# Two graph attention layers: another order of a step's parts in the first layer, and the node update's sum and copies moved

## The chip, the cores and the metric

The kernel runs on one core of a Trainium2 chip. The metric is the device time of one execution in microseconds. The median of three runs of the kernel before is 4821.75 us (4820.29 to 4824.06).

A core has five engines with an instruction queue each: TensorE (PE, matrix products and transposes), VectorE (DVE), ScalarE (ACT), GpSimd (POOL; here it issues the gathers) and SyncE (SP; here it issues all other transfers). In each queue the instructions stand in the order in which the program wrote them, and an instruction that waits for a semaphore holds back all that stand behind it in its queue. The transfers themselves are done by 16 DMA engines.

## The reference, cut to what matters

12500 nodes with 256 features, 200000 edges sorted by their destination, an edge type out of 64.

```python
# layer 0: attention over the incoming edges, 4 heads of 64
enh = x + 0.1 * query_emb
Q, K, V = enh @ Wq + bq, enh @ Wk + bk, enh @ Wv + bv
mod_k = K[src] + 0.2 * rel_w[edge_type]
scores = sum(Q[dst] * mod_k) / 8                 # per edge and head
w = softmax of scores over the edges of one dst
msgs = sum over edges of w * V[src]              # V itself for a node without edges
x1 = layernorm(msgs @ Wo + bo + x) * gamma + beta
x = layernorm(x + x1)
# layer 1: graph attention with a self loop, again 4 heads of 64
xp = x @ W;  a_src, a_dst = per head xp . att_src, xp . att_dst
w = softmax of leaky_relu(a_src[src] + a_dst[dst]) over the edges and the loop of one dst
x = layernorm(x + elu(sum of w * xp[src] + bias))
```

## The kernel before, in words

The kernel has four stages: tables made from the edge list, projection of the nodes to queries, keys and values, `attend_typed` (layer 0) and `attend_plain` (layer 1). The change touches `attend_typed` only.

The edges are cut into 521 tiles of 384 (three chunks of 128; a tile's scores also take the first 32 edges of the next one, the "spill"). A tile has up to 32 destination nodes. Every engine has a loop over steps, and in step t it handles a different part of several tiles. A `TilePart(lag, fn)` in a list calls fn for tile t - lag. The order in which the parts of a step stand in an engine's queue is the order of that list. TensorE's parts are:

- `relate` (lag 0): a one-hot of the edge types times the relation table, into `p_r`.
- `arrive` (lag 1): waits for the three gathers of the tile, then six transposes of key rows into `p_kt` (line 851).
- `turn_weights` (lag 5): transposes the softmax weights (lines 859, 860).
- `score` (lag 3): keys times queries (line 874). It needs the keys of the next tile too, because of the spill.
- `aggregate` (lag 6): weights times value rows (line 889). It frees the tile's row buffer.

GpSimd's `gather` (line 765) issues three indirect transfers per tile into one of eight row buffers. It first waits until `aggregate` of the tile eight places back is done. VectorE's parts are `add_keys` (lines 963, 964: relations added to the turned keys; the keys go to a ring of four tiles), `copy_weights` (line 972, for odd tiles; ScalarE does the even ones), `prepare` (line 980, the one-hot) and `lower_bound` (lines 991, 993: scores less a far mask, and their maximum). ScalarE's are `copy_relations` (1147), `copy_weights` (1155), `set_apart` (1140, the far mask), `weigh` (1160, the exponential) and `put` (1167, the sums to their store). `p_kt`, `p_r`, `p_s`, `p_w` and `p_o` hold one tile each. VectorE's numbers run two steps ahead of TensorE's, ScalarE's one: with TensorE's step s goes VectorE's s + 2.

Beside the tiles, 98 blocks of 128 nodes get their node update. `BlockPart(shift, lag, fn)` calls fn in the step that lies `shift` behind a block's place; the places are 4, 4 and 8 steps apart, three in 16 steps. Block parts stand behind the tile parts of their step. TensorE's part is `update(v)`, which stands ahead of a step's tile parts, one step behind each place. It handles three blocks at once: the output projection of one (lines 902, 904, into `p_out`), the second layer's projection of another (905, 907, into `p_1`), and the transposes of a third's message and a fourth's finished row (915, 917, into `p_message` and `p_x1`). `p_out` and `p_x1` share a bank. VectorE's block parts are `join` (999 to 1005, the message), `sum_up` (1017 to 1024, residual sum and its statistics), `normalize` (1052, 1054), `vary` (1060 to 1065, second statistics), `end_norm` (1073), and the inverse root of three blocks' variances (341 to 348). ScalarE's are `copy_message` (1172), `copy_x1` (1179), `copy_row` (1189 to 1191) and `keep_x1` (1183). After the last tile the block parts run on alone until the last blocks are through.

Of the kernel before, what the change touches and what calls it, by code (L numbers as in the profile page):

```python
# [290 lines left out]
def interleave(eng, first, *parts):  # L291


    assert (TILES - first) % PERIOD == 0

    def step(t):
        for part in parts:
            part.at(t)

    for n in range(first):  # L300
        step(Step(0, n, PERIOD))
    with eng.Fori(0, (TILES - first) // PERIOD) as q:
        for c in range(first, first + PERIOD):
            step(Step(q, c, PERIOD))
    for n in range(TILES, max(part.end() for part in parts)):
        step(Step(0, n, PERIOD))
# [371 lines left out]
def attend_typed(k):  # L678
# [3 lines left out]
    R, M, KEY, SCORE, TURN_LAG, LAG = 8, 4, 1, 3, 5, 6  # L682
    WEIGHTS = 12
    W1 = D + 2 * HEADS
    FIRST = 89
    HALF = PERIOD // 2
    PE_FIRST = 9
    with Stage(nc, "typed") as z:
# [62 lines left out]
        TURN, OUT, TURN1, PROJECT = 2, 3, 10, 11  # L751
# [85 lines left out]
        def _(pe):  # L837
# [55 lines left out]
            def update(v, n, static=False):  # L893


                within = lambda lag: not static or v - lag < ROWS
                pe.wait_ge(row1_ready, v + 1)
                pe.wait_ge(x1_t_ready, v + 1)
                if within(OUT):
                    pe.wait_ge(message_t_ready, v + 1)  # L900
                    pe.wait_ge(summed, v + 1)
                    pe.matmul(p_out, ones[:], bias_o[:], start=True, stop=False)
                    for a in range(2):
                        pe.matmul(p_out, message_t[:, a * P:a * P + P], wo[:, a], start=False, stop=a == 1)
                pe.matmul(p_1, ones[:], bias_1[:], start=True, stop=False)
                for a in range(2):
                    last = pe.matmul(p_1, x1_t[:, a * P:a * P + P], w1[:, a], start=False, stop=a == 1)
                last.then_inc(moved, 1)
                if within(TURN1):
                    pe.wait_ge(x1_ready, v + 1)  # L910
                    if within(TURN):
                        pe.wait_ge(message_ready, v + 1)
                        pe.wait_ge(result_ready, TILES if static else n - LAG)
                        for a in range(2):
                            pe.transpose(p_message[:, a * P:a * P + P], message[:, a * P:a * P + P], ident)
                    for a in range(2):
                        last = pe.transpose(p_x1[:, a * P:a * P + P], x1[:, a * P:a * P + P], ident)
                    last.then_inc(turned_both, 1)

            parts = (TilePart(0, relate), TilePart(KEY, arrive), TilePart(TURN_LAG, turn_weights), TilePart(SCORE, score))  # L920

            def step(t, copied=None):
                for part in parts:
                    part.at(t)
                TilePart(LAG, lambda b: aggregate(b, copied)).at(t)

            pe.wait_ge(setup, 1)
            for n in range(PE_FIRST):
# [25 lines left out]
        def _(v):  # L954
# [52 lines left out]

            def sum_up(b):
                o = b.slot(GROUP)
                v.wait_ge(moved, b.n + OUT + 1)  # L1010
                if not b.known_below(1):
                    back = b.back(-2)
                    if not back.known_below(GROUP):
                        v.wait_ge(inverse, back.use(GROUP))
                if not b.known_below(GROUP):
                    v.wait_ge(normed, b.n - 2)
                v.tensor_tensor(y[:, o], p_out, k.node_rows(b.n), ALU.add).then_inc(summed, 1)
                v.wait_ge(summed, b.n + OUT + 2)
                v.bn_stats(stats[:, 0], y[:, o]).then_inc(stats1, 1)
                v.wait_ge(stats1, b.n + 1)  # L1020
                v.sem_inc(settled3, 1)
                v.bn_aggr(moments[:, 0, o], stats[:, 0]).then_inc(moments1, 1)
                v.wait_ge(moments1, b.n + 1)
                v.tensor_scalar(var[:, 0, o:o + 1], moments[:, 0, o, 1:2], 1e-5, 0.5, ALU.add, ALU.mult).then_inc(var1, 1)
# [95 lines left out]
            for side in range(2):  # L1120
# [4 lines left out]
            v.sem_inc(summed, OUT + 1)  # L1125
            v.sem_inc(x1_ready, TURN1)
            v.sem_inc(setup, 1)
            interleave(v, FIRST, TilePart(KEY + 2, add_keys), TilePart(TURN_LAG + 2, copy_weights), TilePart(0, prepare), TilePart(SCORE + 2, lower_bound),
                       BlockPart(3, 8, end_norm), BlockPart(3, 5, normalize), BlockPart(6, 5, vary), BlockPart(4, 2, sum_up), BlockPart(5, 0, join),
                       BlockPart(7, 0, guess_root, ROWS + 8), BlockPart(8, 0, refine_root, ROWS + 8))  # L1130

        @block.scalar
        def _(act):
# [67 lines left out]
            for lo in range(0, P, REL):  # L1201
                for half in range(2):
# [2 lines left out]
            act.sem_inc(x1_t_ready, PROJECT)  # L1205
            act.sem_inc(row1_ready, PROJECT + 1)
            act.wait_ge(setup, 1)
            interleave(act, FIRST, BlockPart(2, 1, copy_message), TilePart(1, copy_relations), TilePart(TURN_LAG + 1, copy_weights), TilePart(SCORE, set_apart), TilePart(SCORE + 1, weigh), TilePart(LAG + 1, put),
                       BlockPart(4, 10, copy_row), BlockPart(4, 9, copy_x1), BlockPart(5, 8, keep_x1))


def attend_plain(k):
# [1720 lines left out]
```

## Time and profile before

| | us |
|---|---|
| median of 3 runs | 4821.75 |
| the profiled execution's own time | 4847.24 |
| its span | 4845.9 |
| TensorE busy, mean granted clock | 4004.0 (83%), 0.868 |
| VectorE busy | 3436.6 (71%) |
| ScalarE busy | 2781.9 (57%) |
| GpSimd busy | 3127.0 (65%) |
| first and last gather of the first layer | 351.1, 2666.0 |
| first gather of the second layer | 2747.3 |

The shares are means over stages that differ, so a change to one layer is read from that layer's stretch. Busy time of TensorE includes time at half clock, when the same matmul takes longer.

### The profile page before, as it was taken

The page shows a single profiled execution, that of the slowest core. Times are in us where ns is not written, and L with a number is a line of the kernel's source. Part 1 is how long each engine was busy: PE and PEld are TensorE (multiplying, and loading weights), DVE is VectorE, ACT ScalarE, POOL GpSimd, SP SyncE. Part 2 cuts the span into 40 slices and gives each one's busy share as a digit, 9 for nine tenths or more (in the row PEclk, how much of TensorE's full clock was granted, in tenths as well). Part 3 has the DMA queues.
Part 4 walks back from the last instruction along what each step waited for, and adds up shares of the span by engine and source line. Part 5 has one row for each costly group of instructions (what it writes and reads, how often), then busy time and mean ns, then how long its engine had stood idle before and what let it go on. Part 6 is the DMA issues. An engine that isn't in the chain of part 4 may idle for free. (4 is left out here: it accounts for less than half of the span.)

```text
span 4845.9 us, 149801 instructions
## 1 busy us (share of the span) xinstructions
PE 4004.0 (83%) x42462; PEld 2592.5 (53%) x42462; DVE 3436.6 (71%) x11602; ACT 2781.9 (57%) x7985; POOL 3127.0 (65%) x3229
## 2 busy tenths in 40 slices
PE   6978889889998888988889688777788777777785
PEld 4645545555555555555555456555565555555553
DVE  3235667677777777777777568888887787777887
ACT  2324444445454455445545367777777777777775
POOL 1226666666666666666666277777777777777773
PEclk9989999999999999999999677877767887888776
DMA  6878888888888888888888377777777777777774
GB/s 207 282 225 232 236 224 226 231 236 234 235 243 231 234 240 241 231 240 239 232 237 237 101 193 208 206 207 206 208 208 205 207 207 204 204 203 206 205 205 131
DMA packets 820558, 1052.06 MB, mean 217 GB/s; under 512 B 458633, under 2 KB 632338, under 8 KB 820464
## 3 DMA queue, kind: packets, MB, share of 16 engines
q0 software_dynamic: 225072, 726.83, 51.5%
q1 hardware_dynamic: 594078, 323.35, 26.7%
q10 hardware_dynamic: 1314, 0.99, 0.1%
q14 instruction: 80, 0.66, 0.0%
q8 instruction: 14, 0.23, 0.0%
HBM read 915.79 MB, written 133.39 MB: 217 GB/s over the span
## 5 line engine op out<-in xcount | busy, mean ns | idle before, releaser
L765 POOL DMA_INDIRECT typed_rows<-kv,typed_index x1563 | 1491.3, 954 | 857.4 <-PE typed_p_o L889 420.3
L1288 POOL DMA_INDIRECT plain_rows<-xp,plain_index x1563 | 1563.2, 1000 | 556.3 <-issue 437.2
L1140 ACT ACTIVATE typed_far<-typed_match,all_cst 128x416 bf16<-128x416 uint8 x521 | 334.2, 642 | 1002.2 <-DVE typed_col L991 983.8
L1393 PE MATMUL plain_p_o<-plain_rows,plain_weight_t 128*64 128x130 f32 (+1 forms) x8336 | 864.3, 350 | 49.5 <-DVE plain_weight_t L1419 48.8
L1380 PE MATMUL plain_p_s<-all_cst,plain_rows 128*128 128x128 f32 (+1 forms) x2084 | 453.9, 317 | 362.0 <-DMA plain_rows<-xp,plain_index 360.2
L1393 PEld LDWEIGHTS plain_p_o<-plain_rows,plain_weight_t 128*64 128x64 f32 (+1 forms) x8336 | 574.2, 170 | 212.0 <-issue 131.7
L851 PE MATMUL typed_p_kt<-all_cst,typed_rows 128*128 128x128 f32 x3126 | 473.8, 290 | 255.8 <-DMA typed_rows<-kv,typed_index 254.9
L964 DVE TENSOR_TENSOR typed_kt<-typed_p_kt,typed_rel 128x768 f32<-128x768 f32 x521 | 497.0, 954 | 230.7 <-PE typed_p_kt L851 202.2
L1380 PEld LDWEIGHTS plain_p_s<-all_cst,plain_rows 128*128 128x128 f32 (+1 forms) x2084 | 334.9, 173 | 515.1 <-issue 497.4
L851 PEld LDWEIGHTS typed_p_kt<-all_cst,typed_rows 128*128 128x128 f32 x3126 | 345.1, 145 | 359.1 <-DMA typed_rows<-kv,typed_index 299.0
L1426 DVE CUSTOM_DVE_ANT_0 plain_alpha<-plain_alpha,plain_far 128x416 f32<-128x416 f32 x521 | 310.6, 596 | 313.1 <-ACT plain_alpha L1542 299.9
L889 PEld LDWEIGHTS typed_p_o<-typed_rows,typed_weight_t 128*32 128x32 f32 (+1 forms) x16672 | 289.7, 111 | 435.7 <-issue 302.2
L874 PE MATMUL typed_p_s<-typed_kt,typed_q 64*32 64x416 f32 x4168 | 505.5, 558 | 0.0
L1550 ACT ACTIVATE plain_weight<-plain_alpha,plain_col 128x416 f32<-128x416 f32 x521 | 331.6, 636 | 249.5 <-DVE plain_col L1435 242.2
L1561 ACT COPY plain_result<-plain_p_o 32x65 f32<-32x65 f32 x2084 | 423.4, 203 | 18.4
L889 PE MATMUL typed_p_o<-typed_rows,typed_weight_t 128*32 128x65 f32 (+1 forms) x16672 | 427.3, 230 | 1.6 <-ACT typed_result L1167 1.5
L1365 PE MATMUL plain_p_w<-all_cst,plain_weight 128*128 128x128 f32 x1563 | 361.6, 352 | 48.1 <-ACT plain_weight L1550 47.4
L1542 ACT ACTIVATE plain_alpha<-plain_p_s,plain_a_dst 128x416 f32<-128x416 f32 x521 | 316.3, 607 | 124.9 <-PE plain_p_s L1380 102.7
L1419 DVE COPY plain_weight_t<-plain_p_w 128x512 f32<-128x512 f32 x521 | 355.5, 682 | 34.8 <-PE plain_p_w L1366 25.2
L1533 ACT ACTIVATE plain_far<-plain_match,all_cst 128x416 bf16<-128x416 uint8 x521 | 328.6, 631 | 9.1 <-DMA plain_match<-match 9.1
L991 DVE CUSTOM_DVE_ANT_0 typed_weight<-typed_p_s,typed_far 128x416 f32<-128x416 f32 x521 | 305.1, 586 | 39.7 <-PE typed_p_s L874 31.4
L1160 ACT ACTIVATE typed_weight<-typed_weight,typed_col 128x416 f32<-128x416 f32 x521 | 326.3, 626 | 0.6 <-DVE typed_col L993 0.6
(190 smaller groups left out, 6341.7 us busy)
## 6 DMA issues: line engine op xcount, KB each, us to landing
typed_match<-match SPq DMA_DIRECT2D x131, 208.0 KB
plain_match<-match SPq DMA_DIRECT2D x131, 208.0 KB
agg<-qkv_zero SPq DMA_DIRECT2D x98, 264.0 KB
typed_agg<-agg SPq DMA_DIRECT2D x98, 264.0 KB
plain_agg<-agg SPq DMA_DIRECT2D x98, 264.0 KB
kv<-qkv_kv SPq DMA_DIRECT2D x98, 258.0 KB
typed_kinds<-match SPq DMA_DIRECT2D x131, 192.0 KB
typed_rows<-kv,typed_index POOLq DMA_INDIRECT x1563
```

What stands on the lines that cost most here:

```text
L765: pool.indirect_dma_start(rows[:, r, j, :], None, k.kv, bass.IndirectOffsetOnAxis(ap=index[:, g, at:at + 1], axis=0)).then_inc(rows_in[r], 16)
L851: last = pe.transpose(p_kt[:, pair, j * P:j * P + P], rows[:, t.slot(R), j, pair * P:pair * P + P], ident)
L874: last = pe.matmul(p_s[at:at + TN, 0:SLOTS], q[own, m, :, h // 2], kt[own, h // 2, lo:lo + SLOTS], start=True, stop=True, tile_position=(H ...
L889: last = pe.matmul(p_o[at:at + TN, 0:V], weight_t[0:e, t.slot(2), j * P + at:j * P + at + TN], v[:, D + V * h:D + V * h + V], start=j == 0 ...
L964: v.tensor_tensor(kt[:, :, lo:lo + MAIN], p_kt[:, :, 0:MAIN], both_pairs(0, MAIN), ALU.add).then_inc(kt_ready, 1)
L1140: act.activation(far[:], match[:, slab, t.slot(TPB)], ACT.Square, bias=cst[:, C_CODE:C_CODE + 1], scale=FAR).then_inc(far_ready, 1)
L1288: pool.indirect_dma_start(rows[:, r, j, :], None, k.xp, bass.IndirectOffsetOnAxis(ap=index[:, g, at:at + 1], axis=0)).then_inc(rows_in[r], 16)
L1365: pe.transpose(p_w[:, t.slot(2), j * P:j * P + P], weight[:, t.slot(2), j * P:j * P + P], ident)
L1380: last = pe.transpose(p_s[:, c, j * P:j * P + e], a_src[:, A_SRC:A_DST], ident[0:e, 0:e])
L1393: last = pe.matmul(p_o[at:at + HC, t.slot(2), 0:2 * V], weight_t[0:e, t.slot(2), j * P + at:j * P + at + HC], val[:, 2 * V * g:2 * V * g + ...
L1419: v.tensor_copy(weight_t[:, t.slot(2)], p_w[:, t.slot(2)]).then_inc(weight_t_ready, 1)
L1561: last = act.copy(result[at:at + TN, m, 0:V], p_o[at:at + TN, t.slot(2), V * (h % 2):V * (h % 2) + V])
```

## The change

In the first layer the order of the tile parts in a step is another one, on TensorE, VectorE and ScalarE: turned weights, sums, scores, relations, keys. Lags, buffers and instructions are the same. VectorE's block parts stand in another order too, and `end_norm` is one step later. In `update` the wait for the previous row stands behind the output projection. `sum_up` waits for the update's last transposes, where it waited for the second projection. ScalarE copies the turned row (`copy_x1`) ahead of `copy_row`.

```diff
--- before.py
+++ after.py
@@ -894,7 +894,6 @@
 
 
                 within = lambda lag: not static or v - lag < ROWS
-                pe.wait_ge(row1_ready, v + 1)
                 pe.wait_ge(x1_t_ready, v + 1)
                 if within(OUT):
                     pe.wait_ge(message_t_ready, v + 1)
@@ -902,6 +901,7 @@
                     pe.matmul(p_out, ones[:], bias_o[:], start=True, stop=False)
                     for a in range(2):
                         pe.matmul(p_out, message_t[:, a * P:a * P + P], wo[:, a], start=False, stop=a == 1)
+                pe.wait_ge(row1_ready, v + 1)
                 pe.matmul(p_1, ones[:], bias_1[:], start=True, stop=False)
                 for a in range(2):
                     last = pe.matmul(p_1, x1_t[:, a * P:a * P + P], w1[:, a], start=False, stop=a == 1)
@@ -917,12 +917,10 @@
                         last = pe.transpose(p_x1[:, a * P:a * P + P], x1[:, a * P:a * P + P], ident)
                     last.then_inc(turned_both, 1)
 
-            parts = (TilePart(0, relate), TilePart(KEY, arrive), TilePart(TURN_LAG, turn_weights), TilePart(SCORE, score))
-
             def step(t, copied=None):
-                for part in parts:
+                for part in (TilePart(TURN_LAG, turn_weights), TilePart(LAG, lambda b: aggregate(b, copied)), TilePart(SCORE, score),
+                             TilePart(0, relate), TilePart(KEY, arrive)):
                     part.at(t)
-                TilePart(LAG, lambda b: aggregate(b, copied)).at(t)
 
             pe.wait_ge(setup, 1)
             for n in range(PE_FIRST):
@@ -1007,7 +1005,7 @@
 
             def sum_up(b):
                 o = b.slot(GROUP)
-                v.wait_ge(moved, b.n + OUT + 1)
+                v.wait_ge(turned_both, b.n + OUT + 1)
                 if not b.known_below(1):
                     back = b.back(-2)
                     if not back.known_below(GROUP):
@@ -1125,8 +1123,8 @@
             v.sem_inc(summed, OUT + 1)
             v.sem_inc(x1_ready, TURN1)
             v.sem_inc(setup, 1)
-            interleave(v, FIRST, TilePart(KEY + 2, add_keys), TilePart(TURN_LAG + 2, copy_weights), TilePart(0, prepare), TilePart(SCORE + 2, lower_bound),
-                       BlockPart(3, 8, end_norm), BlockPart(3, 5, normalize), BlockPart(6, 5, vary), BlockPart(4, 2, sum_up), BlockPart(5, 0, join),
+            interleave(v, FIRST, TilePart(TURN_LAG + 2, copy_weights), TilePart(SCORE + 2, lower_bound), TilePart(0, prepare), TilePart(KEY + 2, add_keys),
+                       BlockPart(3, 5, normalize), BlockPart(4, 2, sum_up), BlockPart(4, 8, end_norm), BlockPart(6, 5, vary), BlockPart(5, 0, join),
                        BlockPart(7, 0, guess_root, ROWS + 8), BlockPart(8, 0, refine_root, ROWS + 8))
 
         @block.scalar
@@ -1205,8 +1203,8 @@
             act.sem_inc(x1_t_ready, PROJECT)
             act.sem_inc(row1_ready, PROJECT + 1)
             act.wait_ge(setup, 1)
-            interleave(act, FIRST, BlockPart(2, 1, copy_message), TilePart(1, copy_relations), TilePart(TURN_LAG + 1, copy_weights), TilePart(SCORE, set_apart), TilePart(SCORE + 1, weigh), TilePart(LAG + 1, put),
-                       BlockPart(4, 10, copy_row), BlockPart(4, 9, copy_x1), BlockPart(5, 8, keep_x1))
+            interleave(act, FIRST, BlockPart(2, 1, copy_message), TilePart(TURN_LAG + 1, copy_weights), TilePart(LAG + 1, put), TilePart(SCORE + 1, weigh), TilePart(1, copy_relations), TilePart(SCORE, set_apart),
+                       BlockPart(4, 9, copy_x1), BlockPart(4, 10, copy_row), BlockPart(5, 8, keep_x1))
 
 
 def attend_plain(k):
```

## Rows read from the trace of the kernel before

**Rows 1.** Line 851's own view: durations in ns (min/median/max), first and last start.
```profile
L851 PE MATMUL typed_p_kt<-all_cst,typed_rows x3126: 272/273/478, 359.5 to 2675.3; 128*128 128x128 f32 x196
```

**Rows 2.** Stretches of both layers: us, busy us by engine, clock, DMA share, GB/s.
```profile
300.00:2675.00 2375.00, 2090.76 (x28323) 1232.74 (x28322) 1671.49 (x4629) 1139.84 (x2874) 1496.45 (x1570) 0.95 0.82 233
...
2800.00:4846.00 2046.00, 1570.03 (x12289) 1134.18 (x12289) 1610.75 (x6511) 1498.27 (x4682) 1522.72 (x1523) 0.76 0.76 201
```

**Rows 3.** Waits from 400 to 2650 us: who waits for whom, total us, times, longest.
```profile
PE typed_p_kt L851 <- DMA typed_rows<-kv,typed_index: 240.6, 165, 2.9
```

**Rows 4.** Order of time, TensorE: start us, us, engine, line, instructions, idle before.
```profile
1512.37 1.61 PE L874 MATMUL typed_p_s<-typed_kt,typed_q 64*32 64x416 f32 x8
...
1515.02 0.28 PE L902 MATMUL typed_p_t<-typed_bias_o,typed_ones 128*128 128x256 bf16 x1
...
1517.45 0.33 PE L842 MATMUL typed_p_r<-typed_hit,typed_rel_a 128*128 128x384 bf16 x1
...
1521.30 0.87 PE L851 MATMUL typed_p_kt<-all_cst,typed_rows 128*128 128x128 f32 x6
1522.01 0.49 PE L859 MATMUL typed_p_w<-all_cst,typed_weight 128*128 128x128 f32 x3
...
1522.54 0.90 PE L874 MATMUL typed_p_s<-typed_kt,typed_q 64*32 64x416 f32 x8
1523.38 0.79 PE L889 MATMUL typed_p_o<-typed_rows,typed_weight_t 128*32 128x65 f32 x32
...
1524.63 0.88 PE L851 MATMUL typed_p_kt<-all_cst,typed_rows 128*128 128x128 f32 x6
...
1530.34 0.87 PE L851 MATMUL typed_p_kt<-all_cst,typed_rows 128*128 128x128 f32 x6 [2.30 <-DMA typed_rows<-kv,typed_index]
```

**Rows 5.** Stretches again, of 2 us.
```profile
1550.00:1552.00 2.00, 2.00 (x31) 0.66 (x32) 1.29 (x4) 0.00 (x0) 0.99 (x1) 0.50 0.89 292
```

**Rows 6.** Order of time, GpSimd's gathers.
```profile
1521.68 1.15 POOL L765 DMA_INDIRECT typed_rows<-kv,typed_index  x1 [2.30 <-PE typed_p_o L889]
1523.14 0.95 POOL L765 DMA_INDIRECT typed_rows<-kv,typed_index  x1 [0.30 <-issue]
1524.39 0.95 POOL L765 DMA_INDIRECT typed_rows<-kv,typed_index  x1 [0.30 <-PE typed_p_o L889]
```

**Rows 7.** Order of time, VectorE.
```profile
1514.23 0.59 DVE L991 CUSTOM_DVE_ANT_0 typed_weight<-typed_p_s,typed_far 128x416 f32<-128x416 f32 x1 [0.72 <-PE typed_p_s L874]
...
1518.88 0.23 DVE L963 TENSOR_TENSOR typed_kt<-typed_p_kt,typed_rel 128x64 f32<-128x64 f32 x1 [3.87 <-PE typed_p_kt L851]
...
1521.21 0.41 DVE L1073 TENSOR_SCALAR typed_x<-all_x,typed_moments,typed_rstd 128x256 f32 x1
...
1522.58 0.95 DVE L964 TENSOR_TENSOR typed_kt<-typed_p_kt,typed_rel 128x768 f32<-128x768 f32 x1
1523.44 0.68 DVE L972 COPY typed_weight_t<-typed_p_w 128x512 f32<-128x512 f32 x1
1524.04 0.41 DVE L980 TENSOR_SCALAR typed_hit<-typed_kinds,all_cst 128x384 bf16<-128x384 uint8 x1
1524.37 0.58 DVE L991 CUSTOM_DVE_ANT_0 typed_weight<-typed_p_s,typed_far 128x416 f32<-128x416 f32 x1
...
1525.22 0.42 DVE L1017 TENSOR_TENSOR typed_y<-typed_p_t,all_x 128x256 f32<-128x256 f32 x1
...
1526.47 0.15 DVE L1024 TENSOR_SCALAR typed_var<-typed_moments 128x1 f32<-128x1 f32 x1
...
1529.14 0.43 DVE L999 TENSOR_TENSOR typed_agg<-typed_agg 128x264 f32<-128x264 f32 x1
...
1530.03 0.43 DVE L1005 TENSOR_TENSOR typed_message<-typed_agg,typed_share 128x256 f32<-128x256 f32 x1
```

**Rows 8.** Order of time, ScalarE.
```profile
1517.65 0.37 ACT L1172 COPY typed_message_t<-typed_p_o 128x256 f32<-128x256 f32 x1 [1.52 <-PE typed_p_t L917]
```

**Rows 9.** Waits of TensorE from 2675 to 2740 us, the drain.
```profile
PE typed_p_t L902 <- ACT typed_x_t L1179: 8.5, 3, 3.3
```

## The prediction

> **What bounds the kernel now.** I read the page's 40 slices first, then the stretches by stage, then the waits of TensorE, and only then the order of time on each engine. The edits touch the first layer alone. Its transposes of gathered rows begin at 359.5 and end at 2675.3 us, six per tile [rows 1]: 520 steps of 2315.8 / 520 = 4.453 us. In that stage no engine is full: TensorE 2090.8 of 2375 us at a mean clock of 0.95, VectorE 70%, ScalarE 48%, the DMA engines 0.82 [rows 2]. The waits name one thing: 165 times, 240.6 us in 2250 us, the matmuls that transpose gathered rows wait for their gather, never longer than 2.9 us [rows 3]. In 2250 us there are 2250 / 4.453 = 505 tiles, so this is 0.476 us per tile.
>
> TensorE's own step, with nothing late, is from the transposes at 1521.30 to those at 1524.63: 3.33 us, made of transposes 0.71, weights' transposes 0.53, scores 0.84, sums 0.79, and 0.46 left for the relations [rows 4]. A node update adds 1515.02 to 1517.45 = 2.43 us [rows 4], 96 times in the tile loop: 0.45 us per tile. So 3.33 + 0.45 = 3.78 us is work at full clock, 0.48 is waiting, and 4.453 - 4.26 = 0.19 is left. That is the clock: a granted mean of 0.95 of 4.453 us misses 0.22. The scores at 1512.37 take 1.61 us where those at 1522.54 take 0.90 [rows 4], and the stretch from 1550 us runs at 0.50, thus 1.2 GHz [rows 5]; ahead of both, in the order of time, TensorE had waited for rows. About 0.67 us per tile (348 us in all) hangs on late rows.
>
> Why they are late: eight row buffers. The sums of tile s-6 free one, GpSimd then issues three gathers for tile s+2. The gather at 1521.68 was released by the sums, the third went out at 1524.39 [rows 6], and the transposes that used them had to wait 2.30 us until 1530.34 [rows 4], 8.66 us after the first issue. GpSimd needs 3 x 1.25 = 3.75 us for a tile: the two last issues shown lie 1.25 apart. DMA engines: 0.82 x 2375 / 520 = 3.75 us for a tile [rows 2]. So three floors lie together: 3.78, 3.75, 3.75.
>
> **The step order on TensorE: what it gives.** Before, sums come last in a step and the transposes second; between a buffer's release and its need lie 2 steps + relations = 2 x 3.33 + 0.46 = 7.12 us. After, the order is weights, sums, scores, relations, transposes: 3 steps + scores + relations = 9.99 + 0.84 + 0.46 = 11.29 us. The slack grows by 4.17 us, more than the longest wait of 2.9 [rows 3]. If landing gets no slower all of these waits go, and with them the low clock that followed them.
>
> What is late next: the keys. Scores of tile s-3 read the keys of tile s-2. Before, these had a whole step between. After, their transposes end one step and the scores come third in the next, with only 0.53 + 0.79 of TensorE's work between. So TensorE and VectorE hand over once a step: scores, far-masked maximum, hit, keys, scores. The seam from the end of scores (1512.37 + 1.61 = 1513.98) to the maximum at 1514.23 is 0.25 [rows 4, 7]. One round: scores 0.90, seam 0.25, maximum to its last small instruction 0.85 (1524.37 to 1525.22), hit 0.33 (1524.04 to 1524.37), keys 0.95 (1522.58), and the release back, for which I take 0.10, between 0 and that seam's 0.25. Sum 3.38 against 3.33: +0.05 in each of the 520 - 96 = 424 steps that no update covers (in the others 2.43 us cover it): 21 us. Every fourth tile also writes the spill keys, 0.23 more [rows 7]: 130 x 0.23 = 30 us.
>
> **VectorE's order.** The four tile parts cost the same as before; they are only turned so that keys come last. What was free before is not now: node work stands behind the keys and ahead of the next maximum. VectorE is free 0.86 after the keys begin (1522.58 to 1523.44) [rows 7], and the next maximum can begin 0.95 + 0.10 + 0.90 + 0.25 = 2.20 after the same point: a hole of 1.34 us. In it go a copy of turned weights, 0.60 (1523.44 to 1524.04), on every even step, and the node parts. Normalise: 1521.21 to 1522.58 is 1.37 with the end norm, whose own instruction is 0.41, so 0.96; with a copy behind it, 0.22 over the hole. Residual sum with its statistics 1.40 (1525.22 to 1526.62) and now the end norm 0.41: 1.81, no copy, 0.47 over. Join 1.32 (1529.14 to 1530.46) with a copy: 0.58 over [rows 7]. The fourth part, the second statistics, falls beside the update. 1.27 us for each of 98 blocks: 124 us. Bounds: 0, if the edges of the hole are as loose as they were (VectorE has 30% free), and 98 x (0.96 + 1.81 + 1.32) = 401 us plus the copies, if the hole does not exist; I take 124, nearer to the rows of single steps.
>
> **ScalarE, message copy.** Sums in the step behind an update wait for the copied message. Before, everything else of the step covered it. After, only the weights' transposes do, from 1517.45 for 0.53, to 1517.98; the copy runs from 1517.65 to 1518.02 [rows 8] and needs its release: 0.14 late, 96 times, 13 us (bounds 0 and 0.37 x 96 = 36). The other moves on ScalarE cost nothing: its tile work fills 48% of the stage, and its results are due most of a step later. If that cover went, the far mask would be late for the maximum, and every tenth of a us by which it is late would enter the round above: 42 us in 424 steps.
>
> **Update edits.** The residual sum waits for the transposes instead of the projection, later by a part of the update's 2.43 us, but VectorE gets to it a step later anyhow: 0 in the loop. The wait for the previous row moved behind the output projection: 0 in the loop, for the view of [rows 3] lists none of TensorE for that copy. In the drain after the last tile the residual sum no longer queues behind end norm, and turned rows are copied ahead of the row. There three waits for the turned rows hold 8.5 us [rows 9]; I take 5, between 0 and 8.5. SyncE and GpSimd issue the same transfers in the same order; what releases them (sums, scores) comes no later in the step.
>
> **Sum.** Full-clock work 520 x 3.78 = 1965; + 21 + 30 + 124 + 13 = 2153. For rows that still come late I add 20 (0 to 150): at 2153 / 520 = 4.14 us a tile the DMA engines would be 3.75 / 4.14 = 0.90 busy, and 9% of GpSimd is left. 2173 against 2316: 143 less, with the drain 148. The profiled execution took 4847.2 us, its span 4845.9; the median of the runs is 4821.75, 25.5 lower, an offset that I keep. 4847.2 - 148 = 4699 profiled, **4674 us** in plain runs. With the terms at their near bounds this case spans 4600 to 4725.
>
> **Rivals.** (1) Transfers stay the limit. The three floors are 0.03 apart, and a gather issued earlier only stands longer in a queue whose engines are 0.82 busy already. For it: 8.66 us from issue to use is far more than the issues themselves. Against: their share is a mean with idle holes that GpSimd's stalls make. A step of 4.30 (share 0.87) gives 2236, 80 + 5 less: 4737. (2) Nothing moves: ring and handshake cancel at 4.45, about 4817. (3) Slower by the handshake: the seam between scores, keys and scores is paid in each of 424 uncovered steps. The whole gain of 143 us is gone once that round is 143 / 424 = 0.34 us longer than read above; node parts that wait themselves (the join for its sums, the end norm for ScalarE's copy) would do so, as they now stand ahead of the maximum. At 0.55 it adds 233: 2406, 90 more, with the drain 4907. Against: 30% of VectorE is free. (4) Slower by the clock: the long waits become a short stop in nearly every step. The second layer shows that a low clock needs no long stops: TensorE busy 1570 of 2046 us, clock 0.76 [rows 2]. The first layer at 0.88, somewhat over a third of the way from 0.95 to 0.76, would take 2153 / 0.88 = 2447: 131 more, with the drain 4948.
>
> On (4) a page of the Trainium skill speaks against the change: "TensorE: Matmul & The Clock Gate", section "A second HAM failure mode: psum-queue depth-cycling", says that an engine that idles briefly between groups of matmuls often enough goes back and forth between its two clocks. By that rule the time is that of (4). The same page's section on oscillation lays a fall of the clock to waits for transfers, and by that rule the loss goes away with them. The rows of this case bear the second better in this layer (0.50 right behind a wait for rows) and the first in the other layer, hence a small chance.
>
> **Chances.** Forecast 0.55, (1) 0.18, (2) 0.05, (3) 0.13, (4) 0.09. What counts as no change is within 0.2%, 10 us, about what these runs can tell. Faster 0.73, same 0.05, slower 0.22. The range goes from 4600 to 4850: it takes in (1) and (2) and the mild end of (3).
>
> **What would show it.** In the profile after: waits of the row transposes for gathers falling from 0.48 us a tile to below 0.1; the stage's clock at 0.98 or more; a new entry, scores waiting for keys, of some 0.3 us a tile, largest in the steps behind the residual sum and the join; GpSimd's waits for the sums still there but shorter; a step near 4.15 us. It is wrong if row waits stay above 0.3 us a tile (1), if score waits pass 0.7 (3), or if the clock falls below 0.93 without row waits (4).

## The result, and the profile after

The changed kernel takes 4632.49 us in the median (4628.61 to 4632.87, four runs), the kernel before beside it 4822.91 (4820.29 to 4824.4). The ratio is 0.9604, 95% interval 0.9587 to 0.9621: 190 us faster. The forecast was 4674 in a range of 4600 to 4850. The measured gain is 42 us larger than the forecast one. The mechanism held, and several terms of the sum were too large, as shown below.

The first layer's row transposes now run from 359.1 to 2464.1 us, 2105.0 us or 4.048 us for each of 520 steps, where [rows 1] gave 4.453. Line 851's own view of the changed kernel:

```profile
L851 PE MATMUL typed_p_kt<-all_cst,typed_rows x3126: 272/273/475, 359.1 to 2464.1; 128*128 128x128 f32 x196
```

Two stretches of the changed kernel, the first layer and the second, with the columns of [rows 2]. The clock in the first layer is 0.99 (it was 0.95), the DMA engines are 0.88 busy (0.82). The second layer, whose code is the same, takes 2094.0 us from its first gather to the end where it took 2098.6.

```profile
300.00:2464.00 2164.00, 2025.16 (x28362) 1215.09 (x28361) 1650.36 (x4629) 1153.13 (x2875) 1515.60 (x1569) 0.99 0.88 255
...
2536.00:4582.00 2046.00, 1596.13 (x12488) 1153.85 (x12488) 1602.95 (x6446) 1517.01 (x4723) 1557.57 (x1561) 0.76 0.77 204
```

All waits of TensorE from 400 to 2400 us in the changed kernel. No transpose waits for rows any more; in the same window of the kernel before they waited 213.3 us, and [rows 3] has 240.6 us for a longer one. In its place the scores (line 874) wait, 89.4 us in 494 steps, 0.18 us a step.

```profile
PE typed_p_s L874 <- issue: 68.3, 166, 0.8
PE typed_p_s L874 <- DVE typed_kt L962: 21.1, 63, 0.5
```

The second row names VectorE's keys as the releaser. The first has "issue" in its place, and in the order of time below those waits end 0.10 us after the keys are written (that is the median over the 400 to 2400 us). The waits of the second row end 0.35 us after them in the median; nearly all stand in steps with spill keys. What takes the additional 0.25 us no row says.

GpSimd's waits for the sums, kernel before and changed kernel, from 400 to 2400 us. They are fewer and shorter, as forecast:

```profile
POOL typed_rows L765 <- PE typed_p_o L889: 375.6, 263, 3.9
...
POOL typed_rows L765 <- PE typed_p_o L889: 173.7, 200, 2.2
```

TensorE and VectorE of the changed kernel in order of time, from the update of one block on (columns of [rows 4] and [rows 7]; TensorE's line 902 is 901 now, VectorE's lines lie two lower):

```profile
1501.72 0.49 PE L859 MATMUL typed_p_w<-all_cst,typed_weight 128*128 128x128 f32 x3
...
1502.35 0.79 PE L889 MATMUL typed_p_o<-typed_rows,typed_weight_t 128*32 128x65 f32 x32
1503.07 0.90 PE L874 MATMUL typed_p_s<-typed_kt,typed_q 64*32 64x416 f32 x8
...
1506.54 0.90 PE L874 MATMUL typed_p_s<-typed_kt,typed_q 64*32 64x416 f32 x8
...
1510.21 0.91 PE L874 MATMUL typed_p_s<-typed_kt,typed_q 64*32 64x416 f32 x8 [0.27 <-issue]
...
1513.97 0.90 PE L874 MATMUL typed_p_s<-typed_kt,typed_q 64*32 64x416 f32 x8 [0.36 <-issue]
...
1517.85 0.91 PE L874 MATMUL typed_p_s<-typed_kt,typed_q 64*32 64x416 f32 x8 [0.47 <-issue]
...
1521.58 0.90 PE L874 MATMUL typed_p_s<-typed_kt,typed_q 64*32 64x416 f32 x8 [0.32 <-DVE typed_kt L962]
...
1524.92 0.91 PE L874 MATMUL typed_p_s<-typed_kt,typed_q 64*32 64x416 f32 x8
...
1528.41 0.91 PE L874 MATMUL typed_p_s<-typed_kt,typed_q 64*32 64x416 f32 x8
...
1530.49 0.27 PE L901 MATMUL typed_p_t<-typed_bias_o,typed_ones 128*128 128x256 bf16 x1
...
1534.25 0.90 PE L874 MATMUL typed_p_s<-typed_kt,typed_q 64*32 64x416 f32 x8
```

```profile
1505.35 0.22 DVE L961 TENSOR_TENSOR typed_kt<-typed_p_kt,typed_rel 128x64 f32<-128x64 f32 x1
1505.49 0.94 DVE L962 TENSOR_TENSOR typed_kt<-typed_p_kt,typed_rel 128x768 f32<-128x768 f32 x1
...
1509.16 0.95 DVE L962 TENSOR_TENSOR typed_kt<-typed_p_kt,typed_rel 128x768 f32<-128x768 f32 x1
1510.02 0.41 DVE L1015 TENSOR_TENSOR typed_y<-typed_p_t,all_x 128x256 f32<-128x256 f32 x1
...
1511.53 0.41 DVE L1071 TENSOR_SCALAR typed_x<-all_x,typed_moments,typed_rstd 128x256 f32 x1
1511.86 0.58 DVE L989 CUSTOM_DVE_ANT_0 typed_weight<-typed_p_s,typed_far 128x416 f32<-128x416 f32 x1
...
1512.92 0.95 DVE L962 TENSOR_TENSOR typed_kt<-typed_p_kt,typed_rel 128x768 f32<-128x768 f32 x1
```

The round can be read off. Scores at 1503.07 to scores at 1506.54 are 3.47 us: a step with spill keys (1505.35). The next, behind normalise and a copy, is 3.67. The one behind the residual sum (1510.02) and the end norm (1511.53) is 3.76: TensorE sits from the end of its sums until 1513.97, 0.10 after the keys of 1512.92 are written (1513.87). Behind the join it is 3.88. The one from 1517.85 to 1521.58 has the second statistics and spill keys, and is 3.73. A step with little node work, 1521.58 to 1524.92, is 3.34, TensorE's own 3.33. The one with an update, 1528.41 to 1534.25, is 5.84, where 3.33 + 2.43 are 5.76.

The drain after the last row transposes hardly moved: from 2464.1 to the second layer's first gather at 2533.2 are 69.1 us, where from 2675.3 to 2747.3 were 72.0.

### The profile page after: what moved, and what is told of

The parts are those of the page before. It is cut to its first block and busy times, and to the rows that moved or that the text cites. A ratio compares the mean times of both kernels' runs of the same rounds, so it can differ in the third digit from the quotient of the medians.

```text
span 4627.2 us, 149696 instructions
## 1 busy us (share of the span) xinstructions
PE 3929.3 (85%) x42462; PEld 2568.6 (56%) x42462; DVE 3415.2 (74%) x11602; ACT 2795.2 (60%) x7985; POOL 3143.2 (68%) x3229
## 5 line engine op out<-in xcount | busy, mean ns | idle before, releaser
L765 POOL DMA_INDIRECT typed_rows<-kv,typed_index x1563 | 1511.2, 967 | 626.2 <-issue 414.3
L874 PE MATMUL typed_p_s<-typed_kt,typed_q 64*32 64x416 f32 x4168 | 472.4, 521 | 103.4 <-issue 73.0
L851 PE MATMUL typed_p_kt<-all_cst,typed_rows 128*128 128x128 f32 x3126 | 458.4, 283 | 6.8 <-DMA typed_rows<-kv,typed_index 6.3
L889 PE MATMUL typed_p_o<-typed_rows,typed_weight_t 128*32 128x65 f32 (+1 forms) x16672 | 413.4, 225 | 3.0 <-ACT typed_result L1165 0.4
L851 PEld LDWEIGHTS typed_p_kt<-all_cst,typed_rows 128*128 128x128 f32 x3126 | 334.6, 142 | 98.2 <-issue 90.6
L889 PEld LDWEIGHTS typed_p_o<-typed_rows,typed_weight_t 128*32 128x32 f32 (+1 forms) x16672 | 279.6, 108 | 168.2 <-issue 91.1
```

Source lines behind the costliest of these rows:

```text
L765: pool.indirect_dma_start(rows[:, r, j, :], None, k.kv, bass.IndirectOffsetOnAxis(ap=index[:, g, at:at + 1], axis=0)).then_inc(rows_in[r], 16)
L851: last = pe.transpose(p_kt[:, pair, j * P:j * P + P], rows[:, t.slot(R), j, pair * P:pair * P + P], ident)
L874: last = pe.matmul(p_s[at:at + TN, 0:SLOTS], q[own, m, :, h // 2], kt[own, h // 2, lo:lo + SLOTS], start=True, stop=True, tile_position=(H ...
L889: last = pe.matmul(p_o[at:at + TN, 0:V], weight_t[0:e, t.slot(2), j * P + at:j * P + at + TN], v[:, D + V * h:D + V * h + V], start=j == 0 ...
```

## The experiments

Ten of the twelve runs fell on four chips on which the kernel before takes 6018 to 6097 us instead of 4823; whether that is the chip or a condition of it is not known. They are called the slower chips below. The kernel before stands beside each group, and ratios are against it. The last two runs fell on a chip where it takes 4836, called a faster chip like that of the result.

**One: TensorE's order alone.** On the kernel before:

```diff
-                for part in parts:
-                    part.at(t)
-                TilePart(LAG, lambda b: aggregate(b, copied)).at(t)
+                for part in (TilePart(TURN_LAG, turn_weights), TilePart(LAG, lambda b: aggregate(b, copied)), TilePart(SCORE, score),
+                             TilePart(0, relate), TilePart(KEY, arrive)):
+                    part.at(t)
```

> Kernel before with the new order of tile parts on TensorE alone; VectorE and ScalarE keep theirs. Theory of the joint order: VectorE still turns keys ahead of the maximum, so the maximum of a tile waits for transposes that now come after its scores, and p_s is not free before that. From scores: transposes begin 1.3 us on, keys 0.9 later, then 0.87 keys, 0.3 copy (mean), 0.33 hit, 0.67 maximum and its release: the next scores 4.5 us after the last where a step was 3.33. 424 such steps and 96 with an update: 4.7 us a tile, some 4980 us in all, slower than before (4823). Rival, that TensorE's order alone gives the slack and so the gain: 4640 +- 30.

Measured: 7672.78 us, 1.257 of the kernel before (1.2544 to 1.2596). On this kind of chip the whole change loses too, but only 1.7% (f0 below); TensorE's order without VectorE's and ScalarE's is a far larger loss. The direction is as expected, the size was expected at 1.03, and what it would be on a faster chip no run shows. The row transposes run from 359.3 to 4783.5, 8.51 us a step. TensorE's waits from 1000 to 2000 us show a second edge that I had left out: the sums wait for ScalarE's copy of the previous result, which stands last in ScalarE's step, behind an exponential that waits for VectorE.

```profile
PE typed_p_o L889 <- ACT typed_result L1165: 185.8, 96, 2.7
PE typed_p_w L859 <- DVE typed_weight_t L970: 64.0, 37, 1.8
```

The clock is lower too: the same stretch runs at 0.62, where the kernel before on a slower chip (g0) has 0.91.

```profile
1000.00:2000.00 1000.00, 708.31 (x6378) 373.74 (x6378) 376.19 (x1056) 264.82 (x657) 337.34 (x353) 0.62 0.46 123
```

**Two: update edits and block order undone** (run in two groups).

```diff
-                pe.wait_ge(x1_t_ready, v + 1)
+                pe.wait_ge(row1_ready, v + 1)
+                pe.wait_ge(x1_t_ready, v + 1)
...
-                pe.wait_ge(row1_ready, v + 1)
                 pe.matmul(p_1, ones[:], bias_1[:], start=True, stop=False)
...
-                v.wait_ge(turned_both, b.n + OUT + 1)
+                v.wait_ge(moved, b.n + OUT + 1)
...
-BlockPart(3, 5, normalize), BlockPart(4, 2, sum_up), BlockPart(4, 8, end_norm), BlockPart(6, 5, vary)
+BlockPart(3, 8, end_norm), BlockPart(3, 5, normalize), BlockPart(6, 5, vary), BlockPart(4, 2, sum_up)
...
-BlockPart(4, 9, copy_x1), BlockPart(4, 10, copy_row)
+BlockPart(4, 10, copy_row), BlockPart(4, 9, copy_x1)
```

> Changed kernel with the update edits undone: wait for the row ahead of the output projection, residual sum behind the second projection, row copied before the turned row, VectorE's block parts and the end norm's step as before. Theory: the tile order carries all of it; the loop keeps 4.05 us a tile, the drain gives back some 3 to 10 us: 4635 to 4645. Rival, that the end norm's place and the waits matter inside the loop: above 4680.

> Changed kernel with the update edits and the order of VectorE's block parts undone. Against the changed kernel beside it: theory that the tile order carries all of it +3 to +10 us, from the drain; rival, that they matter in the loop: +50 us.

**Three: one row buffer less** (run three times), on the changed kernel.

```diff
-                    pool.wait_ge(agg_done, t.n - R + 1)
+                    pool.wait_ge(agg_done, t.n - R + 2)
```

> Changed kernel, GpSimd waits for the sums of the tile seven places back instead of eight: one row buffer is left unused, nothing else differs. It takes one step (about 4 us) of the 4.17 us of slack that the new order gave. Theory: late rows come back, about 0.4 to 0.5 us a tile on TensorE, and the clock falls behind them: 4780 to 4850. Rival, that the gain came from the order of the handover or the sums and not from the buffers' slack: 4632 +- 15.

> Changed kernel, GpSimd waits for the sums of the tile seven places back instead of eight, so one row buffer is left unused. Against the changed kernel beside it: theory of the buffers' slack +150 to +210 us, with row waits of 0.4 to 0.5 us a tile and a lower clock behind them; rival, that the gain came otherwise: +-15 us.

> Changed kernel, GpSimd waits for the sums of the tile seven places back instead of eight, so one row buffer is left unused: a step of slack less. On a chip where the kernel before takes 4823 us and the changed one 4632: theory of the buffers' slack 4780 to 4850, row waits 0.4 to 0.5 us a tile, clock below 0.98 in the first layer; rival, that the gain came otherwise, 4632 +- 15. On a chip of the other kind (before 6030 to 6100) rows were not awaited and it is to be 1.017 to 1.02 of the kernel before, as in the groups before.

**Four: a longer round**, on the changed kernel.

```diff
+        extra = z.sb("extra", [P, 2, MAIN], U8)
...
+                v.tensor_scalar(extra[:, t.slot(2)], kinds[:, slab, t.slot(TPB), 0:MAIN], cst[:, C_TYPE:C_TYPE + 1], None, ALU.is_equal)
                 v.tensor_scalar(hit[:, t.slot(2)], kinds[:, slab, t.slot(TPB), 0:MAIN], cst[:, C_TYPE:C_TYPE + 1], None,
```

> Changed kernel with one more VectorE pass over the types (128x384, 0.33 us from start to next start, result unused) between the maximum and the keys. Theory: scores, maximum, hit, keys, scores is a round as long as TensorE's step, so it is paid in each of the 424 steps that no update covers: 0.33 x 424 = 140 us, 4770. Rival, that VectorE is 26% free and hides it: below 4660.

**Five: copies on the other parity, the end norm a step earlier**, on the changed kernel.

```diff
# VectorE's copy_weights
-                if t.slot(2) == 0:
+                if t.slot(2) == 1:
                     return
# ScalarE's
-                if t.slot(2) == 1:
+                if t.slot(2) == 0:
                     return
...
-BlockPart(3, 5, normalize), BlockPart(4, 2, sum_up), BlockPart(4, 8, end_norm)
+BlockPart(3, 5, normalize), BlockPart(3, 8, end_norm), BlockPart(4, 2, sum_up)
```

> Changed kernel; VectorE copies the turned weights of even tiles and ScalarE of odd ones (it was the other way), and the end norm stands behind normalise, a step earlier. Theory of the hole of 1.34 us behind the keys: normalise with end norm 1.37 and join 1.32 now stand in steps without a copy and fit, the residual sum 1.40 with a copy is 0.66 over, where 0.22 + 0.47 + 0.58 were over: 0.5 us less a block, 30 to 55 us faster than the changed kernel. Rival, that only the total of VectorE's work counts: +-5 us.

**Six: the changed kernel and the kernel before themselves.**

> The changed kernel itself, as the base of this group. In the group before, the kernel before took 6097 us where it had taken 4823, and three variants of the changed one 6218 to 6232; their traces show TensorE stopping inside a run of eight score matmuls with nothing awaited. Theory: that is the chip's supply of instructions and not the change; where the kernel before takes 4823 this one takes 4632 (ratio 0.960), where it takes 6097 this one takes 6200 to 6240 too. Rival, that the variants themselves were slow: 0.96 on either chip.

> The kernel before once more, for its trace. If this chip is of the kind of the last two groups (some 6030 to 6100 us): theory of the instruction supply says that TensorE stops inside runs of score matmuls here too, with nothing awaited, and a step takes some 5.4 us in the first layer, bound by the number of instructions and not by rows, with row waits below 0.1 us a tile; rival, that late rows are what grew: row waits above 1 us a tile. If it is of the kind of the first (4823 us): the first layer's step is 4.40 to 4.46 us with 0.4 to 0.5 of row waits.

What they measured, all on the slower chips (e, f, g and h are one chip each):

| run | us | kernel before beside it | ratio (95%) |
|---|---|---|---|
| e2, update as before | 6232.17 | 6096.56 | 1.0223 (1.0206 to 1.0240) |
| e3, seven buffers | 6217.67 | 6096.56 | 1.0201 (1.0184 to 1.0218) |
| e4, longer round | 6217.87 | 6096.56 | 1.0204 (1.0187 to 1.0221) |
| f0, changed kernel | 6133.09 | 6030.99 | 1.0168 (1.0146 to 1.0190) |
| f1, seven buffers | 6137.55 | 6030.99 | 1.0186 (1.0161 to 1.0211) |
| f2, update as before | 6148.70 | 6030.99 | 1.0197 (1.0176 to 1.0219) |
| f3, parity and end norm | 6151.33 | 6030.99 | 1.0194 (1.0170 to 1.0218) |
| g0, kernel before | 6043.90 | 6023.18 | one run |
| h1, seven buffers (two runs) | 6144.76 | 6018.28 | 1.0216 (1.0158 to 1.0273) |

So on this kind of chip the same change is 1.7% slower, at the low end of what f0's expectation gave for it (6200 over 6097 is 1.017). The first layer takes (3284.6 - 358.9) / 520 = 5.626 us a step in f0 and (3178.6 - 360.1) / 520 = 5.420 in g0. Line 851's view of both:

```profile
L851 PE MATMUL typed_p_kt<-all_cst,typed_rows x3126: 269/273/477, 358.9 to 3284.6; 128*128 128x128 f32 x196
```

```profile
L851 PE MATMUL typed_p_kt<-all_cst,typed_rows x3126: 269/273/478, 360.1 to 3178.6; 128*128 128x128 f32 x196
```

The matmuls are no slower (273 ns in the median, as before). TensorE stops between them. The second layer, which the change does not touch, is longer on these chips too: from its first gather to the end 2793 us in f0 and in g0, where it takes 2094 and 2099 on the faster one. In order of time in g0, the six transposes of one tile come in pieces after a run of sums, and the stops between pieces wait for nothing:

```profile
1516.13 0.79 PE L889 MATMUL typed_p_o<-typed_rows,typed_weight_t 128*32 128x65 f32 x32
...
1517.65 0.44 PE L851 MATMUL typed_p_kt<-all_cst,typed_rows 128*128 128x128 f32 x2 [0.20 <-DMA typed_rows<-kv,typed_index]
1518.25 0.27 PE L851 MATMUL typed_p_kt<-all_cst,typed_rows 128*128 128x128 f32 x1 [0.16 <-issue]
1518.99 0.27 PE L851 MATMUL typed_p_kt<-all_cst,typed_rows 128*128 128x128 f32 x1 [0.47 <-issue]
1519.72 0.43 PE L851 MATMUL typed_p_kt<-all_cst,typed_rows 128*128 128x128 f32 x2 [0.46 <-issue]
```

In f0 the run that follows the sums is the scores, and it is they that come in pieces; 2.99 us pass from the sums at 1502.24 to the last piece at 1505.23, and VectorE, done with its node work, waits 1.66 us for the scores:

```profile
1502.24 0.79 PE L889 MATMUL typed_p_o<-typed_rows,typed_weight_t 128*32 128x65 f32 x32
1503.00 1.09 PE L874 MATMUL typed_p_s<-typed_kt,typed_q 64*32 64x416 f32 x3
1505.23 0.94 PE L874 MATMUL typed_p_s<-typed_kt,typed_q 64*32 64x416 f32 x5 [1.14 <-issue]
```

Besides, the message copy is late in f0 (the row below is from TensorE's waits from 359 to 3285 us). Its waits take 69.6 us in a layer that is 107 us longer than in g0, where no such wait is listed; that they make up a part of the loss is likely and was not tested. The expectation of g0 had the step (5.4) and the row waits right, but the stops stand in the transposes and sums more than in the scores.

```profile
PE typed_p_o L889 <- ACT typed_message_t L1170: 69.6, 75, 2.0
```

Rows are awaited 5.8 us in 1000 there even in the old order (g0), so there is hardly a late row for the new order to cure. Seven buffers do take the step of slack away: from the first gather of a tile to its transposes pass 17.1 us in the mean in f0 and 11.5 in f1. That is still enough, and the layer is as long, 2926.2 us against 2925.7 (and 2926.3 in h1). So e3, f1 and h1 could not test what they were made for. The longer round, +140 us by my theory, took 6217.87 us where e3 in the same group took 6217.67, and the layers are 2965.8 and 2966.8 long: on these chips the additional pass is hidden, and neither theory of e4 is decided for a faster one.

Undoing the update edits and the block order costs the layer nothing (f2 2925.8 us, f0 2925.7) and the drain 1.2 us (71.5 against 70.3); the median is 15.6 us higher, and nothing in the first layer accounts for that. So on these chips the tile order carries the change in the loop. The predicted gain of 30 to 55 us of f3 did not come there; its layer is 11 us longer. What stops TensorE is not shown. That sums come right ahead of it (32 short matmuls in 0.79 us) fits a supply of instructions that runs dry behind them, and this was only argued.

**Seven: less work for TensorE, in both orders.** The first layer's sums leave out two of a tile's four groups of edges, in `attend_typed`, so these kernels do not compute the reference; gathers and all else stay:

```diff
-                for j in range(CH + 1):
+                for j in (0, CH):
```

> Kernel before, the sums of the first layer leave out two of a tile's four groups of edges: 16 of its 52 matmuls and as many weight loads are gone (0.4 us of matmul time), gathers and all else stay. Theory of the instruction supply, on a chip where the kernel before takes 6030: the first layer's step shrinks by far more than 0.4 us, from 5.42 to 4.2-4.6 us, and then late rows come back as the next limit (0.3 us a tile or more), since between a buffer's release and its need lie 2 x 2.93 + 0.46 = 6.3 us against 8.66. Rival, that matmul time or something in the transfers sets the step: 5.0 us, rows not awaited.

> Changed kernel with the same sums left out. With the supply relieved, the order decides as on the first chip: between release and need lie 3 x 2.93 + 0.84 + 0.46 = 10.1 us, so rows are awaited below 0.05 us a tile, GpSimd's 3.75 us and the round of 3.38 with its block work set 3.9 to 4.3 us a step, and it is 60 to 250 us faster than the kernel before with the same cut. Rival, that the new order loses on this chip whatever the number of instructions: 1.5 to 2% slower than the cut kernel before.

These ran where the kernel before takes 4836.06 us. Both theories were written for a slower chip, so the supply of instructions stays untested; what they say of the order (rows late in the old one, not in the new, 60 to 250 us between the two) is what came. Old order with the cut: 4829.52, ratio 0.9981 (0.9963 to 0.9998). New order with the cut: 4612.59, ratio 0.9532 (0.9510 to 0.9553). Line 851's view of the old order, then of the new:

```profile
L851 PE MATMUL typed_p_kt<-all_cst,typed_rows x3126: 272/273/478, 359.1 to 2675.0; 128*128 128x128 f32 x196
```

```profile
L851 PE MATMUL typed_p_kt<-all_cst,typed_rows x3126: 272/273/478, 360.0 to 2445.8; 128*128 128x128 f32 x196
```

Half of the sums' matmuls are gone, which frees TensorE of 3.33 - 3.10 = 0.23 us in a step with nothing late (transposes at 1508.77 and 1511.87 below). In the old order the stage still takes 2315.9 us, against 2315.8 of [rows 1], and the median is 6.5 us under the kernel before beside it. Hardly any of the freed 120 us arrives. TensorE's work was not the bound; the late rows were. The freed time shows as some more waiting (222.5 us for rows where the uncut kernel has 213.3, and 20 in small waits) and as a lower clock, 0.92 where the uncut kernel has 0.96 in the same window; the new order with the cut has 1.00:

```profile
400.00:2400.00 2000.00, 1752.56 (x17313) 975.82 (x17313) 1427.22 (x3959) 977.80 (x2462) 1289.90 (x1346) 0.92 0.83 234
...
400.00:2400.00 2000.00, 1807.39 (x19230) 1040.88 (x19231) 1571.82 (x4408) 1085.65 (x2745) 1445.71 (x1497) 1.00 0.90 261
```

Order of time in the old order with the cut, a wait for rows and the low clock behind it:

```profile
1508.77 0.87 PE L851 MATMUL typed_p_kt<-all_cst,typed_rows 128*128 128x128 f32 x6
...
1511.87 0.87 PE L851 MATMUL typed_p_kt<-all_cst,typed_rows 128*128 128x128 f32 x6
...
1517.81 1.52 PE L851 MATMUL typed_p_kt<-all_cst,typed_rows 128*128 128x128 f32 x6 [2.76 <-DMA typed_rows<-kv,typed_index]
```

TensorE's waits from 400 to 2400 us, the old order with the cut first, the new one second:

```profile
PE typed_p_kt L851 <- DMA typed_rows<-kv,typed_index: 222.5, 138, 3.2
```

```profile
PE typed_p_s L874 <- issue: 158.3, 349, 1.0
PE typed_p_s L874 <- DVE typed_kt L962: 31.1, 54, 0.8
PE typed_p_kt L851 <- DMA typed_rows<-kv,typed_index: 1.0, 2, 0.6
```

With the same work, the same transfers and the same eight buffers, the old order waits 222.5 us for rows and the new one 1.0, and the two differ by 4829.52 - 4612.59 = 217 us. The two orders differ by the whole change, update edits and block order included; that the tile order is what counts in the loop rests on f2, on a slower chip.

In the new order the score waits are 189.4 us where the uncut kernel has 89.4: most of the freed 0.23 us a step turned into waiting for the keys, and the stage fell by 19 us only, to 2085.8. Sorted by step, the steps with an update fell from 5.84 to 5.62 us, and there are 96 of them. The others did not fall at all: the ones with little node work stay at 3.34 us, though TensorE's own work is down to 3.10. So a round between TensorE and VectorE sets the step wherever no update covers it. This was to be asked by e4, and the cut answers it on a faster chip.

## Why the prediction was right, point by point

**Late rows are the bound, and slack cures them: right, and shown.** The forecast gave 0.48 us a tile of row waits falling below 0.1; there are none after the first tile. The traces show the slack itself. From the first gather of a tile to its transposes pass 9.15 us in the mean in the kernel before and 12.03 in the changed one (tiles 20 to 499). In the kernel before 144 of these 480 tiles kept TensorE waiting for over 0.5 us, and their transposes began 7.0 to 9.3 us after the first gather, 8.1 in the mean: that is how long the three gathers of a tile took to land. In the changed kernel nineteen tiles in twenty are wanted later than 10.4 us after it, and the earliest at 8.5. The pair i1 and i2 shows cause and not only company: less TensorE work changes next to nothing in the old order, and with the same work the new one removes the waits. The direct test, seven buffers on a faster chip, is missing. By these numbers it would leave 12.03 - 4.05 = 7.98 us where landing takes 8.1, so rows should be late again; that is an estimate.

**The clock follows the row waits: right.** 0.95 to 0.99; I had asked for 0.98 or more. Rival (4), many short stops that lower the clock, did not come: the layer stands at 0.99 with 229 score waits of 0.8 us or less in 2000 us of it. In i1 the clock is down again right behind a wait of 2.76 us. What the prediction brought for rival (4) was misread, though. It said that the second layer has a low clock without long stops, from its busy time and clock alone. Its waits for rows, from 2800 to 4500 us of the kernel before, are about as long as those of the first layer and more frequent:

```profile
PE plain_p_s L1380 <- DMA plain_rows<-xp,plain_index: 293.8, 219, 3.8
```

So both layers show a low clock with waits of up to 3 or 4 us for rows, and neither shows one from short stops alone. Why the second layer's is so much lower (0.76 against 0.95) stays open.

**The new wait: right in place, too large in size.** It was put at the scores, for the keys, largest behind the residual sum and the join. I priced round, spill keys, block work and the message copy at 21 + 30 + 124 + 13 = 188 us, with 20 more for rows still late: 2173 us. Measured are 2105.0, so 140 over the 1965 of full-clock work. All steps from 400 to 2400 us, sorted by what VectorE does ahead of the maximum, give where the 140 lie. The excess is over 3.33 us, or over 5.76 in a step with an update.

| step | of 497 | excess, us each | forecast, with the 0.05 of the round |
|---|---|---|---|
| residual sum and end norm | 84 | 0.56 | 0.52 |
| normalise and a copy | 87 | 0.25 | 0.27 |
| join and a copy, no update | 30 | 0.56 | 0.63 |
| spill keys (87 of these with the second statistics) | 125 | 0.27 | 0.28 |
| roots, second step | 30 | 0.17 | 0.05 |
| all others | 48 | 0.03 | 0.05 |
| with an update (62 of these with the join) | 93 | 0.08 | 0.14 |

The price of a step was right nearly everywhere: the forecast's prices with these counts give 144 us for 520 steps, where 140 came. The counts were not. The forecast charged the join, 0.58 us over the hole, in all 98 blocks. But two joins in three stand in a step with an update, whose 2.43 us cover them; that is 39 us too much. A few of the other node parts are covered too, some 6 us. And of the 20 us for late rows none came. These three make up 65 of the 68 us between 2173 and 2105.

**The message copy.** The sums behind an update start 0.63 after the weights' transposes (1501.72 to 1502.35) where 0.53 is their length: 0.10 late, forecast 0.14.

**Drain: 5 us forecast, 2.9 measured.** On a slower chip the same edits were worth 1.2 us there (f2 against f0).

**The offset.** I carried the 25.5 us between the profiled execution of before and the median of its runs over to the changed kernel. Its own profiled execution took 4628.61 us, 4 us under its median. The spans differ by 218.7 us, 210.8 of them in the first layer, 2.9 in the drain and 4.6 in the second layer; the medians differ by 190.4. So in profiled executions the gain was 71 us above my 148, and in plain runs 42: the offset did not hold, and by luck that hid 28 us of the miss. Where in the kernel before the 25 us lay, no run tells.

**Rivals.** (1), transfers as the limit, is out: 0.88 busy and no wait for rows. (2) is out. (3), a round that is 0.34 us longer than read and eats the gain, is out on a faster chip, where the shortest steps are 3.34 us and the round was read as 3.38. It is, though, the nearest to what happened on the slower chips, where stops inside the scores lengthen it and the change loses 1.7%.

## What to carry to other kernels

When a ring of buffers feeds an engine, count the work between the release of a buffer and the need for its next contents, in the order in which the parts stand in the step; putting the releasing part early and the needing part late gave a whole step of slack here without a byte of memory. Then follow what the new order puts next to each other: two engines that hand over once a step must fit the whole round in the step, and work that used to be hidden beside it is paid there. Before such work is charged, look which of it falls into steps that are long for another reason. Move the parts on all engines together: one engine's order alone cost 26% on a slower chip, where the whole change cost 1.7%.

## What the runs showed of the hardware that was not expected

The same program took 4823 to 4836 us in some groups of runs and 6018 to 6097 in others, on four chips. Single matmuls (273 ns for a row transpose), GpSimd's issues of gathers (0.95 us each) and VectorE's instructions last the same; TensorE stops inside runs with nothing awaited, for 0.16 to 1.14 us in the rows above. There the order that gains 4% elsewhere loses 1.7%. A change that shifts slack from one seam to another should be timed on both kinds before it is kept.
